# PSUM banks taken in turn by the token stages, and score rounds of four and three over seven banks in the third attention

## The reference

```python
# block L0 (attention 1, attention 2, MLP)
h = _ln(x) * (1 + sc_msa) + sh_msa
x = x + self_attn_in_windows_of_128(h) * g_msa                # attention 1
h = _ln(x) * (1 + sc_mca) + sh_mca
x = x + cross_attn_over_the_16_best_of_154_keys(h) * g_mca    # attention 2 ("top-k")
h = _ln(x) * (1 + sc_mlp) + sh_mlp
x = x + (silu(a) * b @ w_m2 + b_m2) * g_mlp                   # a, b = halves of h @ w_m1 + b_m1
# block L1 on the x of block L0
x = x + mha(layernorm(x), itself) + t_sa                      # attention 3: full 1024 x 1024 softmax
x = x + mha(layernorm(x), context, mask) + t_ca               # attention 4: 154 keys
x = x + gelu(layernorm(x) @ w1 + b1) @ w2 + b2 + t_mlp
```

## Time and profile before

| | |
|---|---|
| median of 3 runs | 1565.24 us (1562.11 to 1566.72) |
| the profiled execution, own time | 1565.28 us |
| its span, first to last instruction | 1563.5 us |
| mean granted TensorE clock | 0.96 |
| busy: PE, DVE, ACT, POOL | 1395.5, 918.0, 716.2, 341.6 us |

### The profile page before, as it was taken

How to read it: one execution, slowest core, us unless ns; L and a number is a source line. 1 busy time by engine, 2 the same in 40 slices (tenths; PEclk the granted TensorE clock), 3 DMA queues, 4 the chain that set the end, 5 groups by cost and what they waited for, 6 DMA issues and landing times.

```text
span 1563.5 us, 25438 instructions
## 1 busy us (share of the span) xinstructions
PE 1395.5 (89%) x9100; PEld 681.9 (44%) x9100; DVE 918.0 (59%) x2815; ACT 716.2 (46%) x1454; POOL 341.6 (22%) x377
## 2 busy tenths in 40 slices
PE   7999776879889796889899999999999989987898
PEld 5467554444544452342224333333333334543576
DVE  3556397988877785755465666667576235640220
ACT  2255454555465363115544565555455654543221
POOL 0020077766655764000000100000000000010120
PEclk9999988789989898989999999999999999999999
DMA  5200003000000000000002000000000000000000
GB/s 184 67 3 25 19 17 110 9 1 1 4 12 1 28 1 26 0 1 1 1 1 68 1 1 1 2 1 2 1 12 1 1 2 2 13 5 1 14 17 27
DMA packets 22092, 26.74 MB, mean 17 GB/s; under 512 B 4204, under 2 KB 19634, under 8 KB 21708
## 3 DMA queue, kind: packets, MB, share of 16 engines
q1 hardware_dynamic: 21059, 25.03, 5.0%
q10 hardware_dynamic: 909, 0.10, 0.0%
HBM read 21.58 MB, written 3.08 MB: 16 GB/s over the span
## 4 chain that ended last, share of the span: by engine, by line
PE 75%; DVE 10%; ACT 6%; issue 5%; POOL 3%; DMA 1%; SPq 0%; ACTq 0%; POOLq 0%; DVEq 0%
PE bank L1022 27%; PE bank L979 10%; PE bank L1062 8%; PE bank L994 7%; PE bank L958 5%; PE bank L937 3%; PE bank L916 2%; PE bank L964 2%; PE bank L1105 1%; DVE x_hat L1441 1%; PE bank L1086 1%; PE bank L944 1%; DVE left L1496 1%; DVE left L1503 1%; ACT pr L1252 1%
## 5 line engine op out<-in xcount | busy, mean ns | idle before, releaser
L1252 ACT ACTIVATE pr<-bank 128x512 f32<-128x512 f32 x656 | 355.0, 597 | 295.8 <-PE bank L1022 291.7
L1468 DVE TENSOR_REDUCE part_max<-bank 128x1 f32<-128x512 f32 x512 | 327.4, 684 | 210.8 <-PE bank L1022 209.8
L1022 PE MATMUL bank<-slot 32*128 32x512 f32 (+1 forms) x3072 | 398.5, 522 | 10.0 <-ACT pr L1252 5.6
L1022 PEld LDWEIGHTS bank<-slot 32*128 32x128 f32 x3072 | 157.6, 185 | 230.5 <-issue 168.6
L1518 POOL TENSOR_SCALAR var_eps<-mean_var 128x4 f32<-128x4 f32 x24 | 5.5, 230 | 966.1 <-DVE mean_var L1432 966.1
L1574 POOL TENSOR_SCALAR left<-left 128x308 f32<-128x308 f32 x128 | 125.2, 978 | 105.0 <-ACT exp_all L1274 45.3
L979 PE MATMUL bank<-h_t,w_m 128*128 128x512 f32 x256 | 130.8, 635 | 11.9 <-ACT hidden L1228 4.7
L1062 PE MATMUL bank<-pr,v 128*17 128x512 f32 x1024 | 135.6, 601 | 0.0
L1576 POOL TENSOR_TENSOR probs<-left,exp_all 128x308 f32<-128x308 f32 x128 | 107.1, 837 | 10.6
L1493 DVE MAX8 top<-bank 128x8 f32<-128x154 f32 x256 | 69.3, 311 | 42.2 <-PE bank L1086 31.9
L1274 ACT ACTIVATE exp_all<-bank,neg 128x154 f32<-128x154 f32 x256 | 85.5, 386 | 10.1 <-DVE left L1496 5.9
(11 more groups left out here) (140 smaller groups left out, 1779.0 us busy)
## 6 DMA issues: line engine op xcount, KB each, us to landing
w_m<-in_L_xcond_w_m SPq DMA_DIRECT2D x1, 2048.0 KB, 7.9
w_m<-in_L_xcond_w_m SPq DMA_DIRECT2D x2, 1024.0 KB, 8.0
w<-in_L_xcond_w SPq DMA_DIRECT2D x2, 1024.0 KB, 6.3
w_ada<-in_L_xcond_w_ada SPq DMA_DIRECT2D x1, 1792.0 KB, 10.2
x_sb<-in_x SPq DMA_DIRECT2D x6, 256.0 KB, 6.7
res_row<-rows_dram SPq DMA_DIRECT2D x12, 128.0 KB, 3.4
out_x<-x_sb SPq DMA_DIRECT2D x6, 256.0 KB, 2.1
wa<-in_L_xcond_w_qkv SPq DMA_DIRECT2D x1, 768.0 KB, 7.0
```

Source lines behind the costliest of these rows:

```text
L1022: last = nc.tensor.matmul(g.bank(*tile)[:, into], left, right, start=True, stop=True)
L1252: nc.scalar.activation(m.pr[:, u % NPR, :], g.bank("s", gi, i)[:, :], ACT.Exp).then_inc(g.free("s", gi, i), 1)
L1468: nc.vector.tensor_reduce(m.part_max[:, slot, h * TB + i // 8, i // 4 % 2:i // 4 % 2 + 1], bank[:, :], axis=AX.X, op=ALU.max).then_inc(don ...
```

## The change

Four things, all in the plan; no matmul, reduction or copy is added or taken away.

1. In attention 3, from slot `THREES` = 98 to slot 252, the tiles are no longer issued in rounds of four. The two streams of tiles are cut by `FOURS_AND_THREES` into rounds of (2, 2), (2, 1), (2, 2), (1, 2) tiles of kind `s` and `m`: seven tiles in two rounds. `pv` is placed one round later than before.
2. From there on the tiles, and the token steps under them, share banks 0 to 6 (`shares_all`). Before, tiles had six banks and the token steps bank 0.
3. Token stages (2,1), (3,0), (4,0) and, in part, (3,1) no longer prefer bank 0 but take their two or three banks in turn; so do the `ug` steps of stage (6,0), over banks 0 to 6. A preferred bank is now taken only if more than three steps lie behind its last use.
4. The first maxima of attention 4 go in five rounds (three tiles each in the first four) instead of four of four, and start earlier; the first `ug` steps of the last MLP are put earlier, between the last `pv` and `o_turn` steps.

```diff
+THREES = 252 - 7 * 22
+FOURS_AND_THREES = ((2, 2), (2, 1), (2, 2), (1, 2))
...
+def shares_all(step):
+
+    if step[0] in ("m", "s") and attention(step[1]) == 3:
+        return (step[1] - 16 + (step[0] == "s")) * ROUNDS[3] + step[2] // 2 >= THREES + LEAD[3] * (step[0] == "m")
+    if step[0] in ("m_turn", "o_turn"):
+        return (20 if step[0] == "m_turn" else 19) <= step[1] < 24
+    return step[0] in ("on_turn", "y_mm", "hat_turn", "qk", "v") and step[1:3] in ((4, 1), (5, 0))
+
+
 def banks_of(step):
 
     kind = step[0]
+    if shares_all(step):
+        return (0, 1, 2, 3, 4, 5, 6)
     if kind in ("m", "m_turn", "s"):
-        return (3, 4, 5, 6) if attention(step[1]) == 1 else (1, 2, 3, 4, 5, 6)
+        return (3, 4, 5, 6) if attention(step[1]) == 1 else (1, 2, 3, 4, 5) if kind == "m" and step[1] == 16 else (1, 2, 3, 4, 5, 6)
...
 def own_bank(step):
 
-    return attention(step[1]) > 1 if step[0] == "o_turn" else step[1:3] in ((2, 1), (3, 0), (4, 0), (3, 1), (4, 1), (5, 0), (5, 1), (6, 0))
+    if step[0] == "o_turn":
+        return 16 <= step[1] < 19 or step[1] >= 24
+    if step[1:3] == (6, 0):
+        return step[0] in ("on_turn", "y_mm", "hat_turn")
+    return step[1:3] == (5, 1) or step[1:3] == (3, 1) and not first_maxima(step)
...
-                first = banks[0] if step[0] in RING and own_bank(step) and banks[0] in empty else None
+                apart = len(self.steps) - turn.get(banks[0], -9) > 3
+                first = banks[0] if step[0] in RING and own_bank(step) and banks[0] in empty and apart else None
...
+        if a == 3 and THREES <= c < 8 * rounds - lead:
+            stream[0].extend(weighed)
+            stream[1].extend(maxima)
+            while len(stream[0]) + len(stream[1]) >= 7:
+                k = len(begins) - first_three
+                for j in range(2):
+                    n_s, n_m = FOURS_AND_THREES[(k + j) % 4]
+                    tiles = [x for pair in itertools.zip_longest(stream[0][:n_s], stream[1][:n_m]) for x in pair if x]
+                    del stream[0][:n_s], stream[1][:n_m]
+                    round_of(time(THREES + (k + j) * 0.875), width, tiles)
...
+            c += 2 if a == 3 and begins[c] >= time(THREES) and begins[c] < time(8 * rounds - lead) else 1
...
-    for x, (gi, numbers) in enumerate(((24, (0, 1, 2, 3)), (24, (6, 7, 8, 9)), (24, (4, 5, 10, 11)), (25, (0, 1, 2, 3)))):
+    for x, (gi, numbers) in enumerate(((24, (0, 1, 2)), (24, (6, 8, 3)), (24, (7, 9, 4)), (24, (5, 10, 11)), (25, (0, 1, 2, 3)))):
...
-    plan.fill(six[0][0][0], gaps4[20:31])
...
-    plan.spread(six[0][0][1], end + 3, end + 38)
+    plan.fill(six[0][0][0], gaps4[19:30])
+    plan.spread(six[0][0][1], A4 + 16 * R4 - 2.5, end + 38)
```

More of the change, by code:

```diff
@@ L1 @@
+import itertools
 from contextlib import ExitStack
@@ L328, in time, with round_of @@
         return start + first * (min(c, turn) + lead) + then * max(c - turn, 0)
+    def round_of(t, width, tiles, double=False):
+        if tiles:
+            plan.at(t, *tiles, ("scores", *tiles))
+        plan.at(t + 0.3 * width, *[("m_red",) + x[1:] for x in tiles if x[0] == "m"], *[("exp",) + x[1:] for x in tiles if x[0] == "s"])
+        for x in tiles:
+            last_of[x] = len(begins) + double
+        begins.append(t)
+    begins, last_of, stream = [], {}, ([], [])
     for c in range(-lead, 9 * rounds):
@@ L340, in group_run @@
             weighed = [("s", gi_s, i) for i in range(2 * xs, 2 * xs + 4)] if xs % 2 == 0 else []
[L341 to L344, removed]
+        if a == 3 and THREES <= c < 8 * rounds - lead:
[8 more added lines that the diff above has]
+                    round_of(time(THREES + (k + j) * 0.875), width, tiles)
+        else:
+            tiles = [x for both in zip(weighed, maxima) for x in both] if len(weighed) == len(maxima) else maxima + weighed
+            round_of(t, width, tiles, not (weighed and maxima))
+            first_three = len(begins)
@@ L345, in group_run @@
         if c % 2:
             gaps[c] = t + 0.6 * width
[L347 to L356, removed]
+    assert not stream[0] and not stream[1]
@@ new lines, in group_run @@
+    for gi in range((a - 1) * 8, a * 8):
+        c = last_of["m", gi, M_UNITS[a] - 1]
+        t, width = begins[c], begins[c + 1] - begins[c]
+        if a == 3:
+            plan.at(t + 0.5 * width, ("m_neg", gi))
+            plan.at(t + 1.35 * width, ("m_turn", gi), ("m_copy", gi), ("max_rows", gi))
+        else:
+            plan.at(t + 0.9 * width, ("m_turn", gi), ("m_copy", gi), ("max_rows", gi))
+        for d in range(PV_STEPS[a]):
+            c = last_of["s", gi, (d + 1) * S_UNITS[a] // PV_STEPS[a] - 1]
+            c += 2 if a == 3 and begins[c] >= time(THREES) and begins[c] < time(8 * rounds - lead) else 1
+            last = c + 1 >= len(begins)
+            t1 = begins[c] if c < len(begins) else begins[-1] + (c + 1 - len(begins)) * then
+            width = then if last else begins[c + 1] - begins[c]
+            plan.at(t1 + 0.4 * width, ("pv", gi, d))
@@ L357, in group_run @@
             if (d + 1) % (PV_STEPS[a] // 2) == 0:
                 half = (d + 1) // (PV_STEPS[a] // 2) - 1
-                plan.at(t1 + 0.9 * width, ("o_copy", gi_s, half))
-                plan.at(t1 + 1.5 * width, ("o_turn", gi_s, half))
-                plan.at(t1 + 1.9 * width, ("o_norm", gi_s, half))
+                plan.at(t1 + 0.9 * width, ("o_copy", gi, half))
+                plan.at(t1 + 1.5 * width, ("o_turn", gi, half))
+                plan.at(t1 + 1.9 * width, ("o_norm", gi, half))
@@ L528, in make_plan @@
     A4 = end + 0.6 * R4
-    end, gaps4 = last_run(plan, A4, R4, [gaps[c] + 0.1 for c in (267, 271, 275, 279)])
+    end, gaps4 = last_run(plan, A4, R4, [gaps[c] + 0.1 for c in (259, 263, 267, 271, 275)])
     five = joined([gap_slots(5, 1, n) for n in range(2)])
```

15 lines of the change are left out of this document (10 added, 5 removed).

## The result

The changed kernel takes 1524.8 us (median of 4 runs, 1522.8 to 1529.0) beside 1566.0 us for the kernel before on the same chip (4 runs, 1562.1 to 1567.1): ratio 0.9745, 95% interval 0.9718 to 0.9772. That is 41 us less, where 61 were forecast. The time lies inside the range, 21 us above the forecast, and of that 12 us are missing in attention 3 and 10 in the last MLP; the other places differ by less than 2.

A forecast was written before the change was run, and what follows sets the result against it. PE was taken to bound the kernel, its busy time hiding bank waits. Terms -23, -6, -4, -19, -5 and -4 sum to -61 us, from 1565.2 to 1504 us (1494 to 1514 had chance 0.64); range 1492 to 1531.

The forecast's parts named there:

- the rival of the row groups: Attention 3: two tiles on one row group block everything behind, 0.86 us in each of 44 rounds; 1529 us, chance 0.14.
- The bound and the prices: Attention 3: PE bounds; a round costs 0.86 us plus 0.21 per chain, so 176 rounds in 92 chains cost 171.
- Row groups: Attention 3: two tiles of one head in a round cost nothing, except 0.86 us in 4 lone rounds, 3.4 together.
- The first rival: Attention 3: each of 44 rounds with two tiles of one head costs 0.86 us; 1529 us, chance 0.14.
- Token steps in the stretch: Attention 3's recut stretch: token steps' waits for their bank go with seven banks in turn, -10 us.
- the allowance: Attention 3: copies of the 12 qk stand in front of exponentials PE needs sooner, +5 us, between 0 and 12.
- The chains of three: Attention 3: a third round waits for the first round's banks, 0.5, 0.7 or up to 0.9 us late.
- The second rival: Attention 3: readers take the place of banks, costing another 15 to 20 us; 1522 us, chance 0.16.
- The last MLP: Last MLP: ug steps over seven banks -8.3 and -6.8 us, ug 0 to 2 in earlier gaps -3.7; together -19.
- Attention 4's first maxima and attention 4: First maxima in five rounds with seven banks, -6 us; token steps in attention 4 find another bank, -4.
- 590 to 699: From 590 to 699 us: ub and ua waits in bank 0 go, maxima of group 16 wait more; -5 us.
- top-k: Top-k: a 3.2 us ua wait for bank 0 and small ones could go; -4 us, between 0 and -9.

The follow-up runs named there:

- experiment 3: Changed kernel with maxima tiles chosen so that almost no recut round holds two tiles of one head; 1518.6 us, ratio 0.9714.
- experiment 1: Changed kernel with exponentials and maxima's reductions placed directly behind their round in attention 3's recut slots; 1513.8 us, ratio 0.9685.
- experiment 7: Token steps moved inside pairs of rounds, against a kernel with separated heads, early exponentials, new tail and pv only behind whole pairs; 1504.0 us, ratio 0.9606.
- experiment 5: Changed kernel with the edits of experiment 1 and experiment 3 plus a new order of the tail; 1505.6 us, ratio 0.9622.
- experiment 2: Changed kernel with the recut left out: rounds of four and earlier pv in attention 3, seven banks kept; 1519.3 us, ratio 0.9716.
- experiment 4: Changed kernel with hat_turn, modulate and first-half ug steps of the last MLP back at their old times; 1525.6 us, ratio 0.9753.

## Why the prediction was half right

The time lies in the stated range, but not in 1494 to 1514, which had 0.64. It is there because the range reached up to 1531 for the rival of the row groups, which did not come true; that is luck.

- **The bound and the prices** held: PE's chain in the stretch and in the tail, 1.93 for a round of four and one of three, 1.07 for a single one, 171 us as the bare price of the new rounds. For the kernel before, the trace has 47 pairs and 59 single rounds between the two steps (207.1 us) where 49 and 56 were counted (206).
- **Row groups** held. "Loads overtake too", and three of the four single rounds cost 0.7 to 0.85 each; behind the fourth stands a wait that hides the price. The first rival is out (experiment 3). Taking such pairs of tiles out saved 5.3 us (323.0 against 328.3): 2.1 in single rounds, for which 3.4 was in the sum, and 3.1 inside chains, which I had priced at nothing.
- **Token steps in the stretch** held: -11.5, or -10.7 at the same clock, for -10.
- **The failed step** is the allowance: "The copies of the 12 `qk` [...] will now sit in front of exponentials that PE needs sooner: +5 [...] between 0 and 12". Two mechanisms stand in its place. Six rounds had a token step ahead of their exponentials and one `x_hat` ahead of its reductions, 8.8 us (experiment 1, shown). Nine pairs behind a token step found six free banks for seven tiles, 6.8 us, where the prediction let every second round find "three banks that nobody has used since the last chain" (the release by the copy is shown in the trace for the seven behind a `qk`, 5.4 us; for the other two it is argued, and moving the steps, experiment 7, gave only 2 us). Together that is some 16 for 5, beyond the upper bound of 12. Both could have been counted in the order before it ran; I had counted the banks of `scores` steps only.
- **The chains of three** were a little dearer: 0.56 and 1.07 where "0.5", "0.7" and "up to 0.9" stood; with no two tiles of one head in a round the 1.07 is 0.81 (experiment 5).
- **The comparison** with the kernel before misled in one respect: I set the recut against pairs at 2.99 on six banks. On seven banks a pair is 2.86, so 7 of the us that the recut had to bring were to be had by the banks alone (experiment 2).
- **The second rival**, "readers take the place of banks", named the right place; its 15 to 20 us were 12 (its 1522 is the nearest to the 1524.8 measured), but the readers were late by their position in the order, not by their load.
- **The last MLP**, -19, gave -9.3. "-8.3" and "-6.8" for the `ug` steps held: with the tail in its old order the time from `pv` 30,0 to the end falls by 14.5 (166.4 to 151.9, experiment 4). The failed term is "-3.7" for `ug` 0 to 2 under the last `pv` steps. With no time at the lower clock the moved steps cost 0.7 (experiments 1 and 4): `modulate` went ahead of `o_copy`, and `hat_turn` of the second quarter, now only three steps behind its `y_mm`, waits 0.5 us and the `ug` behind it 1.3. The clock took the other 4.5 of this execution.
- **Attention 4's first maxima and attention 4** held within 1 us (-5.5 and -5.0 for -6 and -4). **590 to 699** (-5.9 for -5) would be -4.1 or so in the executions that took 98.3, and **top-k** (-2.3 for -4) is smaller than what the same order differs by, 398.2 to 404.7 us. None of them was tested apart.

What stays open: which executions get the clock's lower level in the tail. The same order had 10.2, 3.4 and 0 us of it, with the same waits ahead.

## What to carry to other kernels

When the spacing of one stream in a planned order changes, look for what now falls between a producer and its reader: an in-order engine that waits for a step issued later holds everything behind it, and this can be counted in the order before anything runs. Count all users of a rotation, not only the main ones: seven banks, seven tiles and one token step make a wait. And price a gain against the best cheap alternative on the same resources (here fours on seven banks), not only against the kernel before.

## What the runs showed of the chip beyond that

The granted clock in the tail fell to 0.5 for 6.8, 3.4 or 0 us with the same instructions and the same idle time ahead, so that the same 48 matmuls took 17.1, 15.5 to 15.8, or 14.2 us. PE had idled for 3.2 us ahead of it in each of these executions. A difference of a few us behind such a place has to be read beside the clock's column before it is put down to the order.
